# The split of Wo into two halves, moved from the first block's groups to the start of the kernel and from VectorE to GpSimd

## What is computed

```python
qkv = hidden_states @ Wqkv
q, k, v = jnp.split(qkv, 3, axis=-1)
q = rope(rmsnorm(q, q_norm_w)); k = rope(rmsnorm(k, k_norm_w))
mask = (q_idx >= k_idx) & (q_idx - k_idx <= WINDOW - 1)
probs = jax.nn.softmax(where(mask, q @ k.T * scale, -inf))
o = (probs @ v).reshape(b, s, h)
x = layernorm(x + o @ Wo)
```

## Time and profile before

| | us |
|---|---|
| median of 3 runs | 1039.35 |
| lowest and highest | 1038.63, 1040.78 |
| the profiled execution, its own time | 1040.8 |
| its span, first to last instruction | 1039.0 |
| TensorE busy in it | 1016.2 |
| VectorE, ScalarE, GpSimd busy | 768.3, 639.3, 444.5 |

### The profile page before, as it was taken

One profiled execution on the slowest core, in us unless ns is written; L12 is line 12 of the kernel. 1 busy time (PEld: TensorE's weight loads), 2 busy tenths in 40 slices (PEclk: granted clock), 3 DMA queues, 4 the chain that ended last, 5 costly groups with the idle time before them and its releaser, 6 DMA issues.

```text
span 1039.0 us, 19736 instructions
## 1 busy us (share of the span) xinstructions
PE 1016.2 (98%) x7088; PEld 838.1 (81%) x7088; DVE 768.3 (74%) x1163; ACT 639.3 (62%) x1310; POOL 444.5 (43%) x537
## 2 busy tenths in 40 slices
PE   7999999999999999999999999999999999999996
PEld 4677777777777777788888888888888888888884
DVE  6888877888888886596766777676677777667465
ACT  4666666666666765333766666666666666766344
POOL 2688888778888852000122222222222222221163
PEclk9999999999999999999999999999999999999999
DMA  5101111111111024735899999999999999999563
GB/s 194 55 23 44 33 33 33 37 51 34 33 44 33 22 84 147 238 91 167 248 260 264 262 272 266 268 264 256 258 281 259 263 266 271 256 249 255 130 209 146
DMA packets 120981, 171.36 MB, mean 165 GB/s; under 512 B 10114, under 2 KB 63746, under 8 KB 120804
## 3 DMA queue, kind: packets, MB, share of 16 engines
q1 hardware_dynamic: 111856, 149.54, 45.2%
q0 software_dynamic: 8736, 20.45, 11.9%
q10 hardware_dynamic: 292, 0.10, 0.0%
HBM read 151.45 MB, written 23.07 MB: 168 GB/s over the span
## 4 chain that ended last, share of the span: by engine, by line
PE 62%; DVE 1%; DMA 1%; ACT 1%; POOL 1%; issue 0%; SPq 0%; POOLq 0%; ACTq 0%; DVEq 0%
PE gate_ps L1614 4%; PE gate_ps L1616 4%; PE gate_ps L1615 4%; PE up_ps L1614 4%; PE up_ps L1616 4%; PE down_ps L1649 3%; PE up_ps L1615 3%; PE down_ps L1651 3%; PE down_ps L1650 3%; PE e_up_ps L1690 3%; PE e_up_ps L1692 3%; PE e_up_ps L1691 3%; PE e_gate_ps L1699 2%; PE e_gate_ps L1701 2%; PE e_gate_ps L1700 2%; PE e_up_ps L1701 2%
## 5 line engine op out<-in xcount | busy, mean ns | idle before, releaser
L1045 POOL DMA_INDIRECT sum_dram<-rows,target_i x39 | 67.0, 1718 | 358.1 <-ACT rows L1156 358.1
L1449 DVE TENSOR_TENSOR e_lo<-e_raw,e_hi 128x1408 fp32r<-128x1408 f32 x78 | 126.8, 1625 | 47.9 <-ACT e_hi L1130 47.8
L1130 ACT CAST e_hi<-e_raw 128x1408 fp32r<-128x1408 f32 x78 | 107.5, 1378 | 50.4 <-PE e_up_ps L1701 49.9
L337 ACT ACTIVATE prob<-score_ps,nbias 128x256 f32<-128x256 f32 (+1 forms) x256 | 118.2, 471 | 5.0 <-DVE nbias L466 5.0
L272 POOL TENSOR_TENSOR probT<-probT,masks 128x256 f32<-128x256 f32 x128 | 91.8, 745 | 55.4 <-DVE probT L496 55.4
L1454 DVE TENSOR_TENSOR ed_lo<-ed_raw,ed_hi 128x1024 fp32r<-128x1024 f32 x39 | 47.8, 1226 | 64.0 <-ACT ed_hi L1138 63.9
L466 DVE TENSOR_REDUCE nbias<-score_ps 128x2 f32<-128x512 f32 (+1 forms) x128 | 86.3, 675 | 4.4
L1051 POOL DMA_INDIRECT rows<-x_dram,token_i x39 | 50.2, 1287 | 88.7 <-DVE target_i L1416 65.1
L344 ACT COPY probT<-probT_ps 128x512 f32<-128x512 f32 x64 | 37.6, 587 | 78.9 <-PE probT_ps L612 78.8
L579 PE MATMUL proj_ps<-wqkv_lo,xT_hi 128*128 128x512 f32 x180 | 78.0, 434 | 1.2 <-ACT squares L358 1.2
L1614 PE MATMUL gate_ps<-x_hi,gu_lo 128*128 128x512 f32 x180 | 72.3, 402 | 0.6 <-DVE gu_lo L1304 0.6
(11 more groups left out here) (283 smaller groups left out, 2973.5 us busy)
## 6 DMA issues: line engine op xcount, KB each, us to landing
e_raw<-in_We_gu SPq DMA_DIRECT2D x78, 704.0 KB, 6.3
ed_raw<-in_We_down SPq DMA_DIRECT2D x39, 512.0 KB, 5.4
raw_ring<-in_Ws_gu SPq DMA_DIRECT2D x58, 256.0 KB, 6.4
wd_raw<-in_Ws_down SPq DMA_DIRECT2D x44, 256.0 KB, 6.5
gu_raw<-in_Ws_gu SPq DMA_DIRECT2D x30, 256.0 KB, 6.2
ed_raw<-in_We_down SPq DMA_DIRECT2D x39, 192.0 KB, 6.8
xT_in<-in_xT SPq DMA_DIRECT2D x16, 256.0 KB, 2.7
x_in<-in_x SPq DMA_DIRECT2D x16, 256.0 KB, 3.1
```

The lines of the kernel that those rows point to most:

```text
L337: nc.scalar.activation(prob[:, g % 2, h, seen], score_ps[:, h, seen], ACT.Exp, bias=nbias[:, s % 2, head:head + 1], scale=1.0, accum_out=r ...
L1130: nc.scalar.copy(e_hi[:, half * HK:(half + 1) * HK, :], raw_half(i, half)).then_inc(e_hi_made, 1)
L1449: nc.vector.tensor_tensor(e_lo[:, part, :], raw_half(i, half), e_hi[:, part, :].bitcast(FP32), ALU.subtract).then_inc(e_lo_made, 1)
```

## The change

The four casts of `split_wo` on ScalarE are issued in the head, between `split_xT(1)` and `take_k(0)`. The four subtracts are issued by GpSimd behind `rms_of(0, 1)` and ahead of the steps, and count on `cleared` instead of `w_lo_made`. Nothing of the split is left in the groups of step 0, on either engine. TensorE waits for `cleared` at s = 1.

```diff
@@ gpsimd_program
+            def split_wo(k):
+                pool.wait_ge(w_hi_made, 6 + k + 1)
+                nc.gpsimd.tensor_tensor(wo_lo[:, k, :], wo_raw[:, k, :], wo_hi[:, k, :].bitcast(FP32), ALU.subtract).then_inc(cleared, 1)
+
             rms_of(0, 0, q_sq, q_var, q_rms)
             rms_of(0, 1, k_sq, k_var, k_rms)
+            for k in range(KT):
+                split_wo(k)
@@ scalar_program
             split_xT(1)
+            for k in range(KT):
+                split_wo(k)
             take_k(0)
             take_v(0)
 
             for s, g in steps():
                 a, n = s + 1, 4 * s + g - 1
-                if s == 0:
-                    split_wo(g)
@@ vector_program
-            def split_wo(k):
-                dve.wait_ge(w_hi_made, 6 + k + 1)
-                nc.vector.tensor_tensor(wo_lo[:, k, :], wo_raw[:, k, :], wo_hi[:, k, :].bitcast(FP32), ALU.subtract).then_inc(w_lo_made, 1)
@@
-                if s == 0:
-                    split_wo(g)
                 if g == 3 and has(s + 2):
                     split_xT(s + 2)
@@ tensor_program
                     if s == 1:
-                        wait(pe, w_lo_made, 6 + KT)
+                        wait(pe, cleared, 5 + KT)
```

## The result

The changed kernel takes 1041.44 us in the median of 9 runs (1040.47 to 1044.08), the kernel before 1039.20 us in 9 runs beside them (1038.43 to 1040.78). The ratio is 1.0027 with a 95% interval of 1.0018 to 1.0036: slower by 2.2 us in the medians. The ratio does not go by the medians; it lies near that of the means, 1041.98 and 1039.23, which are 2.75 us apart. The forecast was 1041.0 us, the range 1039.0 to 1043.0. Of the three classes the forecast's likeliest was "within 0.2%". Its bound was 1041.4, and the median lies 0.04 us beyond it, in the class that had 0.38; so small a step over the bound says nothing.

A forecast was written before the change was run, and what follows sets the result against it. TensorE was taken to bound the kernel, busy 1016.2 of 1039.0 us. Removal 0, casts 0 and GpSimd's subtracts +1.6 us on the median 1039.35 gave 1040.95, stated as 1041.0 us, range 1039.0 to 1043.0.

The forecast's parts named there:

- Landing of Wo, casts on ScalarE, cost 0: Head: Wo landed at 17.1 us, four casts run 19.84 to 22.05 within ScalarE's 3.21 us wait; cost 0.
- The handovers in the head: Head: GpSimd's subtracts and VectorE's two-SBUF-input instructions take turns, delaying lines 204 and 446; first scores +1.30 us.
- rival 2: Head: GpSimd gets in one turn earlier, ahead of line 202; first scores +2.6 us, 1042.0 us; chance 0.12.
- the turn changing at the record's end: Head: lock taken to the letter, handing over at the record's end instead of 0.13 us before; +1.9 instead of +1.3.
- The fourth subtract: Head: ties with VectorE's line 471; hidden if VectorE is first, +0.64 us if GpSimd is, +1.94 in all.
- The removal is worth 0: Step 0 groups: taking out casts and subtracts gives back 0, with bounds of 0 and -2.34 us.
- Rival 1, the clock: Head: TensorE's half clock lasts over v's second half; first scores +2.8, up to +3.5, 1041.9 to 1042.9 us; chance 0.13.
- The row that I held against it: From 34 to 37 us TensorE was busy only 1.79 of 3.0 us and kept the full clock.
- The sum: Whole change: +1.6 us, the middle of three outcomes, +1.30, +1.94 and +1.66; chance of +1.3 to +1.95 was 0.52.
- Carried to the end one for one: Before 46 us: whatever is given or taken reaches the end fully, since TensorE never stands still later for the head.
- The margin between "same" and "slower": Whole kernel: slower means above 1041.4 us, about 0.2% (2.1 us); chances 0.38 slower, 0.59 within 0.2%.

The follow-up runs named there:

- the version with both waits: Changed kernel, GpSimd's Wo subtracts waiting for k's rotation and its first mask products for q's rotation of block 1; median 1038.13 beside 1039.14 us, ratio 0.9992.

## Why the prediction was right or wrong

- *Landing of Wo, casts on ScalarE, cost 0*: right. They take 2.18 us for four, and 1.49 us of cover is left.
- *The handovers in the head*: right, nearly to the tenth. Forecast were 1.7 us for line 204 and 2.3 for line 446, measured 1.66 and 2.29; the second half of v was to start 2.1 us late (2.04), the first scores 1.30 (1.32). The order of turns was the forecast one in all three profiles, and rival 2, GpSimd ahead of line 202, did not occur. In the six handovers up to line 473 the new owner's full duration fits in from 0.13 to 0.15 us before the old one's record ends. The sum with the turn changing at the record's end was given as +1.9 (four handovers of 0.13 us make it 1.8); measured is 1.32, so the tenth that the rows showed was right.
- *The fourth subtract*: of the two outcomes, +1.30 and +1.94, the second came in all three profiles (1.80 to 1.82 us for the remainder of xT). I had called it a tie, and GpSimd was ahead by 0.01 to 0.02 us each time. Taking a middle of 1.6 between outcomes that exclude each other made the sum some 0.3 us too small: this is the term that was mis-sized. The experiment with three subtracts in the head measured it alone: 0.65 us against the forecast 0.64.
- *The removal is worth 0*: right, 0.08 us, and for the reason given: VectorE's earlier rotation stands behind GpSimd's mask product (1.07 us for line 193). The experiments with the mask product held back show the other half of it, 0.6 us.
- *Rival 1, the clock*: its size was near where it occurred, +2.6 us to the first scores (forecast +2.8) and +3.1 and +3.8 to step 1 (up to +3.5), with run times of 1042.9 to 1044.1 for the three timed ones (1041.9 to 1042.9). But I gave it 0.13 as a case of the whole kernel, and it is one of single executions: it comes on top of the collision, by the granted clock in three of nine timed runs, and in two of three profiled ones. The row that I held against it was a wait of TensorE in group 2 that did not cost the clock, but that came out of a stretch at the full clock; here the waits fall into one at half. Why it stays down in some executions and not in others is open.
- *The sum*: forecast 1.6. Without the long half clock step 1 comes 1.85 us later than in the first profile of before and 2.05 later than in the second, and the means of the runs differ by 1.99: it is the forecast's upper outcome, +1.94. The three runs with the long half clock raise the median from 1041.30 to 1041.44 and the difference of the means to 2.75.
- *Carried to the end one for one*: right between executions of one kernel. Those of the changed kernel differ by 1.22 and 1.96 us at step 1, and from 50 us on the distance between their timelines stays within 0.15 us of where it was then. Between the two profiles of the kernels it can't be read, since the three jumps of 0.6 us take the 1.85 back; there the means of the runs, 1.99 us apart, have to stand for it.
- *The margin between "same" and "slower"*: the median of 1041.44 is on the bound of 1041.4, and on which side it fell is chance.

## What to carry to other kernels

A move from a busy engine to an idle one has to be judged by what the two engines share, not by their busy shares. Here GpSimd was idle for 6.9 us. But its subtracts and products of SBUF tiles took turns with VectorE's instructions that have two SBUF inputs, each turn for a whole instruction, and 5.1 us of GpSimd's work put 3.2 us into three VectorE instructions. So list VectorE's instructions in the gap by where their inputs lie. Those with one input in PSUM kept their 0.68 us beside GpSimd's subtracts, and those with two SBUF inputs kept theirs beside GpSimd's memsets. One wait, which let the last instruction of k's rotation go first, took the cost to step 1 from 1.85 us down to 0.2. And look for the same collision at the place where the freed time is to be used, or it is eaten there.

## What the runs showed that I had not expected

- A few hundredths of a microsecond in the order of two instructions decide 0.6 us, in single blocks: a GpSimd instruction of 128x1 (0.55 us) issued 0.03 us behind a VectorE subtract takes 1.06 us, and TensorE pays 0.6. It happened three times in one profile of before and twice in the other, and not once in three profiles of the changed kernel. Over all profiles it happened 13 times in the seven executions without subtracts on GpSimd in the head and twice in the seven with them, so the change may have a part in it. The run times speak against it: if the change took these collisions away for good, the kernels would differ by less than the 1.85 to 2.05 us of the head, and without the long half clock they differ by 1.99 in the mean.
- The half clock at the start of the changed kernel lasted 3.4 us in one execution and 10.2 us in two, with the instruction order the same. In the two TensorE waited 1.09 us while already at half clock, and in the slower one 0.64 us ahead of that; the kernel before has no such wait there, and its half clock lasted 3.4 us both times. But the version with both waits had 6.8 us of it in one of two executions without such a wait.
- The version with both waits on GpSimd gave the lowest ratio (0.9992, with a median of 1038.13 against 1039.14 beside it) and the narrowest spread of the kernels timed, 1.4 us.
